# A two-layer graph network's edge loop: two gathers in one step, the second add into M a step later, the zeros of M at other places

## The reference

```python
src, dst = edge_index
edge_feat = concatenate([x[src], x[dst], edge_attr], axis=-1)
h = mish(edge_feat @ W1 + b1)
messages = mish(h @ W2 + b2)
agg = segment_sum(messages, dst, num_segments=1250)
u = mish(concatenate([x, agg], axis=-1) @ W3 + b3)   # then W4, layer norm
# second layer: support = x @ U * s @ Vt
output = segment_sum(support[src] * edge_weight[:, None], dst, 1250)
```

## Time and profile before

| | us |
|---|---|
| median of 3 runs (1515.99 to 1518.47) | 1516.13 |
| profiled execution, its own time | 1518.77 |
| its span, first to last instruction | 1517.1 |
| TensorE busy in it | 1489.8 |
| DVE, ACT, POOL busy | 1411.0, 1302.0, 1079.7 |
| granted TensorE clock, mean | 0.997 |

### The profile page before, as it was taken

How to read it: one execution, slowest core, us unless ns; L and a number is a source line. 1 busy time by engine, 2 the same in 40 slices (tenths; PEclk the granted TensorE clock), 3 DMA queues, 4 the chain that set the end, 5 groups by cost and what they waited for, 6 DMA issues and landing times.

```text
span 1517.1 us, 33370 instructions
## 1 busy us (share of the span) xinstructions
PE 1489.8 (98%) x7862; PEld 1167.1 (77%) x7862; DVE 1411.0 (93%) x2920; ACT 1302.0 (86%) x2510; POOL 1079.7 (71%) x978
## 2 busy tenths in 40 slices
PE   7989999999999999999999999999999999999998
PEld 6767777777777777777777777777777777777885
DVE  7888999999999999999999999999999999996676
ACT  5088999999999999999999999999999999996562
POOL 1266888888888888887888888888878888863320
PEclk9999999999999999999999999999999999999999
DMA  8784555455455545444554545454455555554773
GB/s 288 269 280 107 122 123 125 112 131 116 118 122 123 122 115 129 116 118 118 125 118 115 125 123 121 118 125 118 115 123 123 123 117 126 115 135 102 176 166 148
DMA packets 124756, 205.10 MB, mean 135 GB/s; under 512 B 31641, under 2 KB 57369, under 8 KB 124720
## 3 DMA queue, kind: packets, MB, share of 16 engines
q0 software_dynamic: 58528, 112.91, 34.5%
q1 hardware_dynamic: 65840, 91.24, 19.3%
q10 hardware_dynamic: 352, 0.52, 0.1%
HBM read 151.60 MB, written 42.75 MB: 128 GB/s over the span
## 4 chain that ended last, share of the span: by engine, by line
PE 82%; DVE 5%; issue 4%; DMA 4%; POOL 2%; ACT 1%; POOLq 1%; DVEq 0%; SPq 0%; ACTq 0%
PE bm L1158 49%; PE bp L1137 7%; PE bp L1145 5%; PE bs L1181 4%; PE bp L1147 4%; DMA xg<-A_tab,idx 2%; PE pm L1169 2%; PE po L2146 2%; PE pu L336 2%; PE pu L2124 2%; PE pm L1168 1%; POOL hTl L1063 1%; DMA A_tab<-ta 1%; DVE bm L1350 1%; PE pu L2191 1%
## 5 line engine op out<-in xcount | busy, mean ns | idle before, releaser
L1063 POOL TENSOR_TENSOR hTl<-tp,hTh 128x512 fp32r<-128x512 f32 (+1 forms) x314 | 413.0, 1315 | 204.0 <-DVE khl L1357 203.2
L1158 PE MATMUL bm<-W2h,hTh 128*128 128x512 f32 x1252 | 498.3, 398 | 1.2 <-DVE bm L1350 0.8
L1158 PE MATMUL bm<-W2l,hTh 128*128 128x512 f32 x1252 | 496.7, 397 | 0.0
L1158 PE MATMUL bm<-W2h,hTl 128*128 128x512 f32 x1252 | 494.6, 395 | 0.0
L1050 POOL DMA_INDIRECT xg<-A_tab,idx x305 | 321.6, 1054 | 65.3 <-issue 37.7
L1158 PEld LDWEIGHTS bm<-W2h,hTh 128*128 128x128 f32 x1252 | 235.4, 188 | 71.0 <-DVE bm L1350 15.8
L1158 PEld LDWEIGHTS bm<-W2l,hTh 128*128 128x128 f32 x1252 | 235.4, 188 | 57.4
L1158 PEld LDWEIGHTS bm<-W2h,hTl 128*128 128x128 f32 x1252 | 235.5, 188 | 53.7
L1217 ACT ACTIVATE rp<-bp 128x512 f32<-128x512 f32 (+1 forms) x314 | 183.7, 585 | 107.1 <-PE bp L1147 77.3
L1321 DVE SCALAR_TENSOR_TENSOR rp<-rp 128x512 f32<-128x512 f32 (+1 forms) x314 | 214.8, 684 | 36.9 <-ACT rp L1217 17.5
L1331 DVE SCALAR_TENSOR_TENSOR tp<-rp,bp 128x512 f32<-128x512 f32 (+1 forms) x314 | 211.6, 674 | 4.7 <-ACT rp L1223 2.4
(11 more groups left out here) (248 smaller groups left out, 2306.6 us busy)
## 6 DMA issues: line engine op xcount, KB each, us to landing
ea<-in_eaT SPq DMA_DIRECT2D x156, 128.0 KB
M_tab<-mev POOLq DMA_DIRECT2D x157, 80.0 KB, 5.7
agg_tab<-ev POOLq DMA_DIRECT2D x157, 64.0 KB, 2.5
db<-in_dst_rows SPq DMA_DIRECT2D x78, 128.0 KB
M<-M SPq DMA_DIRECT2D x76, 128.0 KB
M_tab<-zero SPq DMA_DIRECT2D x10, 640.0 KB
xg<-A_tab,idx POOLq DMA_INDIRECT x313
eaW<-Bh_tab SPq DMA_DIRECT2D x77, 64.0 KB
```

What stands on the lines that cost most here:

```text
L1063: e.tensor_tensor(hTl[p][:, j, 0:w], pick(u, start_t, tp)[:, 0:w], hTh[p][:, j, 0:w], ALU.subtract)\
L1158: last = e.matmul(bank[0:r, :], a[p][:, c, j * P:j * P + r], w[:, c, :], start=False, stop=c == KC - 1 and w is W2l, skip_group_check=True)
```

## The change

The four gathers of a group go out in residues 2, 3 and 0, the last two together. Half 1 of M's add moves from residue 0 (lag 8) to residue 1 (lag 9), where it stands behind the first agg add. For group 0, half 0 is left out of step 6 and issued in step 9 directly ahead of half 1, and the wait for the zeros moves there. On SyncE four zeros are issued between the window rows and the copy of group 2, one behind the loads of group 3, and five between the window rows and the copy of group 4; group 4 is written out, group 5's loads too, and the loop starts at group 6.

```diff
-    GATHER_AHEAD = {2: (10, (0,)), 3: (9, (1,)), 0: (8, (2,)), 1: (7, (3,))}
+    GATHER_AHEAD = {2: (10, (0,)), 3: (9, (1,)), 0: (8, (2, 3))}
-    ADJ_LAG = {2: (6, 0), 0: (8, 1)}
+    ADJ_LAG = {2: (6, 0), 1: (9, 1)}
@@ SyncE, behind window_rows(At(None, 8))
-            for i in range(3):
+            for i in range(4):
                 zero_m(e, i, q_zlate)
             window_copy(At(None, 8))
-            indices(At(None, 12))
-            for i in range(3, 5):
+            loads(At(None, 12))
+            zero_m(e, 4, q_zlate)
+            indices(At(None, 16))
+            features(At(None, 16))
+            targets(At(None, 16))
+            window_rows(At(None, 16))
+            for i in range(5, NCH):
                 zero_m(e, i, q_zlate)
-            features(At(None, 12))
-            targets(At(None, 12))
-            window_rows(At(None, 12))
-            for i in range(5, 8):
-                zero_m(e, i, q_zlate)
-            window_copy(At(None, 12))
-            for i in range(8, NCH):
-                zero_m(e, i, q_zlate)
-            with e.Fori(2, FULL // 2) as i:
+            window_copy(At(None, 16))
+            loads(At(None, 20))
+            with e.Fori(3, FULL // 2) as i:
@@ POOL, step(s)
                     lag, half = ADJ_LAG[s.j]
-                    if (s + -lag).has(4 * FULL):
-                        if half == 0 and s.reg is None and s.const == lag:
-                            e.wait_ge(q_z, 16 * ZERO_DMAS)
+                    u = s + -lag
+                    if u.has(4 * FULL) and not (half == 0 and u.reg is None and u.const == 0):
+                        if half == 1 and u.reg is None and u.const == 0:
                             e.wait_ge(q_zlate, 16 * NCH)
-                        adjacency(s + -lag, half)
+                            adjacency(u, 0)
+                        adjacency(u, half)
```

## The result

The change made the kernel slower, by 0.4%. After: 1524.12 us, median of 7 runs (1521.59 to 1524.8); before, beside it: 1516.72 us, median of 7 (1515.99 to 1518.47). The ratio is 1.0044, 95% interval 1.0032 to 1.0055. The profiled execution of after took 1524.12 us, its span is 1522.4.

The account below looks back on a forecast made before the run. TensorE, busy 1489.8 of 1517.1 us, was taken as the bound. Terms -3.4 - 3.67 + 1.6 + 0.75 = -4.72 took 1518.77 to 1514.05; the median's 2.64 lower gave 1511.4 us, range 1508.5 to 1516.5.

Parts of the forecast that it names:

- the tail's: After the loop: the last second M add moves behind the agg add that waits for DVE; cost 0.
- rival 3: Steady loop: second M add lands too late for the next group's first; 0.6 us a group, about 1557 us; chance 0.04.
- Steady gather waits, -3.4: Steady loop: the fourth gather, issued 2.2 us earlier, removes all 7 TensorE waits for gathers, 3.4 us.
- The first bound given for this term, 0: Steady loop: no gain from the earlier gather if the holds do not occur in executions without the profiler.
- The start, -3.67: Loop's start, step 7: the 2.16 us gather wait and 1.51 us of slow clock go; bounds 2.2 and 3.7.
- the signs that were asked for: Loop's start: step 7 within 0.1 us of the segment product's end; granted clock 1.00 over 110 to 125 us.
- The transfer of the sum to the median by one constant difference (2.64): Whole kernel: the median lies 2.64 us below the profiled execution's time, so 1514.05 becomes 1511.4 us.
- The pair of adds, +1.6 + 0.75: Loop's start: group 0's two M adds in step 9 make TensorE wait 1.6 us, plus 0.75 for the clock.
- 3.4 to 4.5 foretold: Loop's start: POOL's second M add of group 0 stands 3.4 to 4.5 us behind the first.
- chain of nine spans: Loop's start: POOL's work from step 9 to the subtraction of step 11, for which TensorE waits 1.2 us in step 12.
- The zeros at cost 0: Loop's start: five zeros behind group 4's window rows are done by 123.7, before POOL asks at 128.3; cost 0.

Follow-up runs that it names:

- M's adds alone: The kernel before with only the second M add moved to lag 9, behind the first agg add; 1523.39 us, ratio 1.0043.
- the tail taken back: The kernel after, with the second M add back at lag 8 in residue 0 in the steps written out after the loop; 1517.69 us, ratio 1.0005.
- the later loads: The kernel after, with SyncE's loads of V3 and the first ag tile (1 MB each) issued 16 us later; 1519.02 us, ratio 1.0010.
- the run with one DMA fewer: The kernel before without M's second adds, so seven POOL DMAs a group and not eight, M left wrong; one run, 1514.89 us.
- The spread gathers: The kernel before with the second gather issued one step earlier, beside the first in residue 2; 1515.73 us, ratio 0.9984.
- the run with the adds a step apart: The kernel after with the old lag in the tail and group 0's M adds in steps 8 and 9, not both in 9; one run, 1515.62 us.
- the start alone: The kernel before with SyncE's zeros at their new places and group 0's two M adds together in step 8; 1522.18 us, ratio 1.0040.
- the gathers alone: The kernel before with only the gathers' places changed, third and fourth in one step; 1516.76 us, ratio 1.0002.

## Why the prediction was wrong

**The step that failed is the tail's: "M is read only once the last group's adds, later still, have landed. Cost 0."** It asked who reads M, and not who stands behind the add on its own queue. Putting half 1 a step later puts it one step ahead of the next group's first M add, which waits for its landing with POOL's subtraction behind it. The prediction had this mechanism as rival 3 and cleared it for the steady loop, rightly: the landing there fits. It had even read its row right: "5.7 looks like the one add that met the big loads at the end". That is the last add, at 1404.80 us. The moved one, issued at 1359.08, met two other loads and took 7.84 us, above the 5.1 from which rival 3 decides; that loads at the end lengthen a landing was known, and was not carried over to it. The rival was priced by 77 groups at 46 us and given 0.04; once, with the clock's fall behind it, it costs 6.39, and 1.91 in the node stage. The runs of M's adds alone, of the tail taken back and of the later loads show it from three sides. The 6.39 and the 1.91 together are more than the whole distance from the forecast to no change. They aren't all of the miss: with the tail taken back the time was 1517.69, still above the range, because the next term isn't there either.

**Steady gather waits, -3.4: measured 0,** the second step that failed. The waits went, as said. But a pause of POOL is not made shorter by what it issues first. Where the fourth gather no longer catches it, the agg add, M add and subtraction do. One of the three in after, in POOL's, DVE's and TensorE's timelines:

```profile
609.91 0.90 POOL L1076 DMA_DIRECT2D agg_tab<-ev  x1 [2.28 <-issue]
611.33 0.93 POOL L1087 DMA_DIRECT2D M_tab<-mev  x1 [0.51 <-issue]
611.96 1.62 POOL L1062 TENSOR_TENSOR hTl<-tp,hTh 128x512 fp32r<-128x512 f32 x1
```

```profile
611.73 2.00 DVE L1311 TENSOR_TENSOR oh<-iota_w,drel 128x128 f32<-128x128 f32 x1
```

```profile
616.91 0.50 PE L1158 MATMUL bm<-W2h,hTh 128*128 128x512 f32 x1 [0.92 <-DVE bm L1350]
```

The agg add starts 2.28 us after POOL's last work (1.19 at the median over the groups), the subtraction slides into DVE's L1311, which takes 2.00 us where 0.40 is usual, and TensorE starts 0.92 us late. Three such groups (1.14, 1.27 and 1.14 us over the median group) and the small rest make 4.24 us of excess over 72 median groups. Before had 4.24 us too, 3.8 of it in seven groups. That the two are equal to a hundredth is chance (1196.76 to 1198.03 in the other runs with these places of M's adds and gathers); that they are near is not: only the run with one DMA fewer won it back. The spread gathers lost the excess too, but every group was longer. The first bound given for this term, 0, was the right value, for a reason that the prediction did not name.

**The start, -3.67: measured -3.78** (2.30 and 1.48 from the table) against that profiled execution, and the signs that were asked for are there: no wait at step 7, clock 1.00 throughout 110 to 125 us. Right by its steps. But 1.51 of it was the clock's fall, which three of five executions do not have; against the four other executions with the old start it gives 1.7, 2.4, 2.6 and 3.5 us. The transfer of the sum to the median by one constant difference (2.64) probably counted that part twice: the two later executions of before, whose times (1516.54 and 1517.0) are near the median, had no fall to remove. The unprofiled runs can't show it.

**The pair of adds, +1.6 + 0.75: measured +1.92,** without a fall of the clock, and by another path from POOL to TensorE. The second add stands 3.55 us behind the first, 3.4 to 4.5 foretold:

```profile
127.03 0.94 POOL L1087 DMA_DIRECT2D M_tab<-mev  x1 [0.20 <-issue]
130.58 0.84 POOL L1087 DMA_DIRECT2D M_tab<-mev  x1 [2.61 <-DMA M_tab<-mev]
131.15 1.60 POOL L1062 TENSOR_TENSOR hTl<-tp,hTh 128x512 fp32r<-128x512 f32 x1
```

But TensorE does not wait for the subtraction of step 11, as the prediction's chain of nine spans had it. The late subtraction of step 10 (131.15) runs beside DVE's L1337, which takes 2.21 us where 0.42 is usual, and TensorE waits for DVE (DVE's and TensorE's timelines of after):

```profile
130.83 2.21 DVE L1337 CAST hTh<-tp 128x512 fp32r<-128x512 f32 x1
...
134.65 0.50 PE L1158 MATMUL bm<-W2h,hTh 128*128 128x512 f32 x1 [1.29 <-DVE bm L1350]
```

The three runs with the pair in step 9 (after, the tail taken back, the later loads) have this one long L1337 each, and no other; before and the run with the adds a step apart have none. So the size of this term came out near for a reason that the prediction did not have, which is luck.

**The zeros at cost 0:** held together with the early gather, and only so, as the start alone showed. The pair is part of their price: the gathers alone, with the zeros at their old places, have the shorter start.

With the traces' values the sum is: start -1.7 to -3.5, steady 0, pair +1.9, tail +6.4, node stage +1.9, so 1516.7 + 6.7 to 8.5 = 1523.4 to 1525.2 where 1524.12 was measured. This is bookkeeping of the profiled execution, not a second proof. Of the versions run, the one with the second gather beside the first, and nothing else changed, is the best: 0.9984 of before.

## What to carry to other kernels

When a DMA with a landing wait behind it is moved, follow it through the loop's last turns as well, and set its landing there against what the next stage has just begun to load; a long landing in a list is a warning about every place with such loads, and it pays to see which of the DMAs it was. A wait in TensorE's list names the instruction at which a delay of another engine arrives; unless the edit gives that engine time back, the delay arrives elsewhere. And before a gain is added up from one profiled execution, ask which of its stalls the median has.

## What the runs showed of the hardware

- POOL pauses by 0.5 to 1.5 us at places that hardly move: in before and in after one series comes every 12 groups (199 us) and one about every 15 (250 us), near the same times. With the gathers alone changed the first series and the second's pause at 349 us stand out, with the gathers spread neither series does. No row names their cause.
- An M add of 80 KB that waits for the landing of the one ahead of it stands 3.55 us behind it in the start; in the tail the landing took 7.84 us with 2 MB of loads just ahead, and with the loads later the second add stood 3.86 us behind the first.
- DVE's L1311, with two SBUF inputs, is slowed by POOL's subtraction beside it. In the steady stretch it takes 643 ns in the mean after the change, 405 before; at the median over the groups the subtraction runs beside it for 0.46 us, 0.25 before. The group of DVE's instructions in after:

```profile
L1311 DVE TENSOR_TENSOR oh<-iota_w,drel 128x128 f32<-128x128 f32 x73 | 47.0, 643 | 0.0
```

  The Trainium skill (GPSIMD Engine Reference, Specifications) says that POOL shares its SBUF interfaces with VectorE and contends with instructions that have two SBUF inputs or run in a 2-port perf mode. The trace agrees for L1311: 2.00 us for 0.40 at 611.73, while the subtraction of 611.96 runs. L1337 has one input and took 2.21 us for 0.42 at 130.83; in which mode it runs no row shows.
- TensorE's clock fell after gaps of 1.76 and 2.16 us (both at step 7), 3.13 us (tail) and 4.48 us (the start alone), and not after 1.76, 2.35 and 2.59 us at step 7. So the length of the gap alone did not tell.
